# Joint value-output weights split on TensorE and ScalarE, reciprocals moved ahead, in a two-layer gated cross-attention kernel

## The chip, the cores and the metric

The kernel runs on one core of one Trainium2 chip as a single launch. The metric is device time in microseconds (us), the slowest core's, which here is the only one. A core has TensorE (PE, whose weight loads are listed apart as PEld), VectorE (DVE), ScalarE (ACT), GpSimd (POOL) and SyncE (SP), each with its own instruction stream, and DMA queues. They order each other by semaphores.

## The reference, cut to what matters

Two layers of gated cross-attention and feed-forward follow each other on x of shape (16, 128, 256). The change lies in the attention of the second layer:

```python
def _L1_xattn_ref(x, latents, ...):      # x = ctx_1024, latents = layernorm(x of the block)
    B, M, N, DIM, DH, H = (8, 1024, 64, 256, 128, 8)
    xn = _layernorm(x, gamma_media, beta_media)
    ln = _layernorm(latents, gamma_lat, beta_lat)
    q = ln @ Wq + bq
    kv = concatenate([xn, ln], axis=1) @ Wkv + bkv
    k, v = split(kv, 2)
    ... 8 heads of 128, q scaled by 128 ** -0.5
    attn = softmax(q k^T)
    return (attn v).reshape(b, -1, 1024) @ Wo + bo
x = x + tanh(g_xattn[1]) * _L1_xattn_ref(ctx_1024, layernorm(x), ...)
```

The actual batch is 16 with 128 queries and 256 keys (128 of the context, 128 of x). The kernel does not make v: since attn (t Wv) Wo = (attn t)(Wv Wo), it multiplies Wv and Wo once per head into joint weights of 256 x 256 (`nw`), weighs the normed tokens t by attn, and multiplies the result u by the joint weights. The bias of v goes through Wo once and is added to bo.

## The kernel before, in words

All large products take their operands as a high part rounded to the short float format of TensorE (type fp32r) and a low part, which is the remainder, so three matmuls (high high, high low, low high: `PARTS3`) stand for one.

**The entry block** (L1492 to L1553) runs between two barriers of all engines. TensorE multiplies the turned value weights with the raw output weights, two matmuls per head, into one of three PSUM banks `psN` (L1505). ScalarE first rounds the key weights (L1511), then copies each head's product twice: rounded into `nw[0]` (L1514), and whole into `made_nw` (L1515). VectorE scales and splits the query weights (L1531 to L1533), takes the low part of the key weights (L1536), adds the routed rows of the first two batches to x (`combine`, L1469), takes their statistics and norms (`norm_step`, L66 to L95, 15 steps of tiny operations in a chain), and writes the normed rows (L1548, L1552). GpSimd waits for the last stores of the feed-forward before, gathers four batches' rows by indirect DMA (L1465), and then widens the value bias, `bvw` (L1524).

**The main block** works on 8 pairs of batches with 8 heads each, so 64 units, and is software-pipelined by a hand-written order: in step n TensorE does `keys(n)` (L1646), `score(n-1)` (L1665), `queries(n)` (L1655), in the first steps two heads of `values_bias` (L1712), in some steps `turn_kv` of a coming batch (L1637), `output(n-5)` (L1705), `weigh(n-4)` (L1686) and `turn(n-2)` (L1675), the transposes of the probabilities. Step 4 has no `output` yet. Both `turn_kv` and `turn` write the one PSUM bank `psT`, so `turn` waits until the low part of what `turn_kv` left there has been read (`kv_lo`):

```python
def turn(n, turned_kv):
    pe.wait_ge(s["p_done"], n + 1)
    at_least(pe, s["pt_lo"], n)
    at_least(pe, s["kv_lo"], turned_kv)
```

The steps in which this happens are written out in tables; a step counts within its pair (n modulo 8):

```python
NORM_AT, TURN_AT, TOKENS_AT = {2: 0, 4: 1}, {4: 0, 6: 1}, {5: 0, 7: 1}
```

VectorE's order in step n is: low part of k (`keys`, L1872); row maximum of unit n-1 (L1882); low part of q (L1877); in steps 0 to 3 two `lower_product` each, which write `nw[1]` = `made_nw` - `nw[0]` (L1947); in step 3 `sum_bias` (L1952, L1954); in steps 2 and 4 of each of the first seven pairs `later_norm`, which norms a batch of the next pair by four operations of two SBUF inputs (L1475, L1480); in steps 4 and 6 `stage_kv`, the low part of the turned rows (L1867); `normalize(n-1)`, the reciprocal of the exponentials' sums (L1887); `weigh(n-4)` (L1897) and `turn(n-2)` (L1892), again low parts; and last the entering of further batches (L1469, L1921, and links of the norm chain). Each of these waits for its own semaphore, and what stands behind it waits too.

ScalarE's order is high part of k (L1761), of q (L1765), the two exponentials of unit n-1 with their sums (L1771), tokens (L1756), `stage_kv` (L1749), and the high parts of u (L1783) and of the turned probabilities (L1778). GpSimd multiplies the probabilities by the reciprocals (L1833) after VectorE's reciprocal, and gathers, adds the bias to x (L1839) and lowers tokens (L1824) in other steps.

## Time and profile before

| what | value |
|---|---|
| median of 3 runs | 1040.09 us |
| lowest and highest | 1036.69 and 1044.4 us |
| the profiled execution's own time | 1037.69 us |
| its span, first to last instruction | 1035.9 us |
| what lies around the span | 1.79 us |
| mean granted TensorE clock | 0.961 |
| TensorE busy | 943.9 us, 91% |
| VectorE busy | 735.7 us, 71% |
| ScalarE busy | 615.9 us, 59% |
| GpSimd busy | 301.6 us, 29% |

The entry block takes about 319.6 to 333.6 us of the span and the attention's main block 333.6 to about 762 us. Busy shares are means over stages; a stage's own limit is read from its waits. A granted clock of 1.00 is TensorE's upper level, 2.4 GHz, and 0.50 its lower one, 1.2 GHz. In the timeline rows a line has the start, the duration, engine, line of the program, operation, what it writes and reads, shapes and the count of instructions merged in it; a bracket holds the time that the engine sat idle before it and what ended that.

### The profile page before, as it was taken

The page shows a single profiled execution, that of the slowest core. Times are in us where ns is not written, and L with a number is a line of the kernel's source. Part 1 is how long each engine was busy: PE and PEld are TensorE (multiplying, and loading weights), DVE is VectorE, ACT ScalarE, POOL GpSimd, SP SyncE. Part 2 cuts the span into 40 slices and gives each one's busy share as a digit, 9 for nine tenths or more (in the row PEclk, how much of TensorE's full clock was granted, in tenths as well). Part 3 has the DMA queues.
Part 4 walks back from the last instruction along what each step waited for, and adds up shares of the span by engine and source line. Part 5 has one row for each costly group of instructions (what it writes and reads, how often), then busy time and mean ns, then how long its engine had stood idle before and what let it go on. Part 6 is the DMA issues. An engine that isn't in the chain of part 4 may idle for free. (4 is left out here: it accounts for less than half of the span.)

```text
span 1035.9 us, 22000 instructions
## 1 busy us (share of the span) xinstructions
PE 943.9 (91%) x7942; PEld 870.8 (84%) x7942; DVE 735.7 (71%) x1812; ACT 615.9 (59%) x1500; POOL 301.6 (29%) x361
## 2 busy tenths in 40 slices
PE   5899999777997899999999999999988999799993
PEld 4688876776886689999999999999877999799992
DVE  7888888685778878776666565655667876565655
ACT  4688886474987355555555555555555443566560
POOL 3444434035002334222222222131100002466631
PEclk9899999888998899999999999999999999899997
DMA  9511110014731101000000000020051001454417
GB/s 276 197 54 53 64 63 2 1 36 123 210 113 50 39 21 47 1 22 9 14 21 1 22 1 22 1 74 30 2 163 42 1 2 22 118 167 135 132 56 269
DMA packets 64617, 69.24 MB, mean 67 GB/s; under 512 B 11488, under 2 KB 56032, under 8 KB 64384
## 3 DMA queue, kind: packets, MB, share of 16 engines
q1 hardware_dynamic: 57680, 52.22, 16.1%
q0 software_dynamic: 5712, 15.36, 5.4%
q8 instruction: 65, 1.06, 0.4%
q10 hardware_dynamic: 1120, 0.27, 0.1%
q14 instruction: 40, 0.33, 0.1%
HBM read 46.07 MB, written 21.76 MB: 65 GB/s over the span
## 5 line engine op out<-in xcount | busy, mean ns | idle before, releaser
L1833 POOL TENSOR_TENSOR a_probs<-a_probs,a_softmax 128x512 f32<-128x512 f32 x64 | 66.7, 1043 | 296.2 <-DVE a_softmax L1887 296.2
L1646 PE MATMUL a_psK<-a_kvThi,a_wk 128*128 128x512 f32 x256 | 97.4, 421 | 2.5 <-DVE a_klo L1872 2.5
L1897 DVE TENSOR_TENSOR a_ulo<-a_psU,a_uhi 128x512 fp32r<-128x512 f32 x64 | 44.2, 691 | 66.7 <-ACT a_uhi L1783 66.7
L314 POOL TENSOR_SCALAR t_neg<-t_raw,t_nthr 128x256 bf16<-128x256 f32 (+1 forms) x54 | 60.5, 1136 | 103.6 <-DVE t_nthr L557 97.6
L1771 ACT ACTIVATE a_probs<-a_psS,a_softmax 128x256 f32<-128x256 f32 x128 | 59.5, 470 | 34.9 <-DVE a_softmax L1882 34.9
L2420 POOL DMA_INDIRECT rows<-m_tokens,r_comes x40 | 40.4, 1009 | 125.4 <-DVE r_comes L2630 109.8
L1686 PE MATMUL a_psU<-a_pThi,a_tokhi 128*128 128x256 f32 x256 | 72.8, 284 | 2.3 <-DVE a_pTlo L1892 2.3
L1705 PE MATMUL a_psY<-a_nwhi,a_uhi 128*128 128x256 f32 x256 | 73.4, 287 | 1.2 <-DVE a_ulo L1897 1.2
L1686 PE MATMUL a_psU<-a_pThi,a_toklo 128*128 128x256 f32 x256 | 72.4, 283 | 0.0
L1686 PE MATMUL a_psU<-a_pTlo,a_tokhi 128*128 128x256 f32 x256 | 72.4, 283 | 0.0
L1761 ACT ACTIVATE a_khi<-a_psK,a_bk 128x512 fp32r<-128x512 f32 x64 | 44.0, 688 | 47.7 <-PE a_psK L1646 47.4
L1705 PE MATMUL a_psY<-a_nwlo,a_uhi 128*128 128x256 f32 x256 | 72.3, 282 | 0.0
L1705 PE MATMUL a_psY<-a_nwhi,a_ulo 128*128 128x256 f32 x256 | 72.1, 282 | 0.0
L2316 PE MATMUL f_psY<-a_wk,f_g_split 128*128 128x256 f32 x480 | 67.3, 288 | 3.0 <-issue 2.3
L1783 ACT ACTIVATE a_uhi<-a_psU 128x512 fp32r<-128x512 f32 x64 | 38.2, 597 | 52.8 <-PE a_psU L1686 52.1
L1872 DVE SCALAR_TENSOR_TENSOR a_klo<-a_psK,a_bk,a_khi 128x512 fp32r<-128x512 f32 x64 | 47.7, 746 | 25.5 <-ACT a_khi L1761 25.5
L2303 PE MATMUL f_psH<-m_turned,a_wq 128*128 128x320 f32 x384 | 65.5, 318 | 0.0
L2316 PEld LDWEIGHTS f_psY<-a_wk,f_g_split 128*128 128x128 f32 x480 | 59.9, 188 | 4.8 <-issue 3.8
L2673 DVE TENSOR_TENSOR f_g_split<-f_g,f_g_split 128x320 fp32r<-128x320 f32 x64 | 30.4, 490 | 42.1 <-ACT f_g_split L2372 33.3
L1646 PEld LDWEIGHTS a_psK<-a_kvThi,a_wk 128*128 128x128 f32 x256 | 48.9, 191 | 12.7 <-DVE a_klo L1872 3.6
L2366 ACT ACTIVATE f_g<-f_psH,f_xb 128x320 f32<-128x320 f32 x64 | 33.0, 528 | 44.6 <-PE f_psH L2303 33.4
L1765 ACT ACTIVATE a_qhi<-a_psQ,a_bq 128x256 fp32r<-128x256 f32 x64 | 30.3, 473 | 48.3 <-PE a_psQ L1655 48.3
(412 smaller groups left out, 3191.8 us busy)
## 6 DMA issues: line engine op xcount, KB each, us to landing
t_raw<-in_L_ffn_expert_w SPq DMA_DIRECT2D x16, 512.0 KB, 3.5
f_raw<-in_fc_T SPq DMA_DIRECT2D x16, 512.0 KB
m_results<-a_zeros SPq DMA_DIRECT2D x8, 512.0 KB, 3.5
m_sorted<-m_zeros SPq DMA_DIRECT2D x1, 2944.0 KB, 12.6
m_n<-m_sorted SPq DMA_DIRECT2D x23, 128.0 KB, 2.3
m_expert_out<-e_y SPq DMA_DIRECT2D x23, 128.0 KB, 1.7
a_rawkv<-in_L_xattn_Wkv SPq DMA_DIRECT2D x8, 256.0 KB, 5.6
m_n<-in_sh_T SPq DMA_DIRECT2D x2, 1024.0 KB, 8.5
```

The source lines that it names most:

```text
L314: ins = pool.tensor_scalar(neg[:, own], raw[h % NRAW][:, own], nthr[h % 2][:, n:n + 1], None, ALU.is_lt)
L1646: ins = pe.matmul(psK[:].rearrange("p b t -> p (b t)"), wk[x][:, a, h * DH:(h + 1) * DH], kvT[pair % 2][y][:, a, :, :, :].rearrange("p b m ...
L1686: ins = pe.matmul(psU[b][:, f, :], tok[pair % 2][x][:, b, kt, f * P:(f + 1) * P], pT[gr % 2][y][:, b, kt, :, :].rearrange("p h t -> p (h t)"),
L1705: ins = pe.matmul(psY[:, b, :], u[ch % 2][x][:, f, hh * P:(hh + 1) * P], nw[y][:, f, 2 * j + hh, :], start=first, stop=last, skip_group_ch ...
L1761: act.activation(k_[n % 2][0][:], psK[:], ACT.Identity, bias=bk[:, n % NH:n % NH + 1]).then_inc(s["k_hi"], 1)
L1771: act.activation(probs[n % 2][:, b, :], psS[n % 2][:, b, :], ACT.Exp, bias=nmax[:, n % NM, b:b + 1], accum_out=sums[:, n % NM, b:b + 1]).t ...
L1833: pool.tensor_tensor(own, own, rsum[:, n % NM, :].unsqueeze(2).to_broadcast([P, 2, 2 * P]), ALU.mult).then_inc(s["p_done"], 1)
L1872: dve.scalar_tensor_tensor(out=k_[n % 2][1][:], in0=psK[:], scalar=bk[:, n % NH:n % NH + 1], in1=k_[n % 2][0][:].bitcast(F32), op0=ALU.add ...
L1897: dve.tensor_tensor(u[ch % 2][1][:], psU[ch % 2][:], u[ch % 2][0][:].bitcast(F32), ALU.subtract).then_inc(s["u_lo"], 1)
L2303: ins = pe.matmul(psH[k % NG][:, 0:HALF], xw1[e % 2][x][:, a * F + f * P:a * F + (f + 1) * P], xT[e % 2][y_][:, a, rows], start=(n == 0), ...
L2316: ins = pe.matmul(psY[n % 2][:, 0, :], xgs[e % 2][x][:, f, t * P:(t + 1) * P], xw2[e % 2][y_][:, f * D:(f + 1) * D], start=(k == 0), stop= ...
L2420: pool.indirect_dma_start(xin[e % 2][:, t, :], None, xr, bass.IndirectOffsetOnAxis(ap=comes[:, e * NT + t:e * NT + t + 1], axis=0))\
```

## The change

1. In the entry block ScalarE copies each head's product once, rounded (`upper`), TensorE then adds minus that high part to the same PSUM bank (`take_off`, one matmul of 128x512 with `less`, the negated identity, as weights), and ScalarE copies the remainder into `nw[1]` (`lower`). `made_nw` and VectorE's eight `lower_product` are gone, and with them the waits for `n_lo`. VectorE makes `less` as its first instruction.
2. GpSimd widens the value bias ahead of the gathers rather than behind them, and TensorE does the first two heads of `values_bias` at the end of the entry block; the others move one step ahead, so `psY` is allocated earlier.
3. In VectorE's steps the reciprocal `normalize(n-1)` stands directly behind the low part of q, ahead of `sum_bias`, `later_norm` and `stage_kv`.

```diff
@@ -1482,12 +1482,23 @@
             ins.then_inc(normed, 1)
             dve.wait_ge(normed, n)
 
+        psY = ps("a1_psY", [P, 2, D], F32, c)
+        psB = psY[:, 0, :]
         with ExitStack() as r:
             rawq, rawkv, rawo = (begun["weights"][n] for n in ("q", "kv", "o"))
-            made_nw = sb("a1_made_nw", [P, KD, NH, D], F32, r)
+            spare = sb("a1_spare", [P, KD * NH * D - P], F32, r)
+            less = sb("a1_less", [P, P], F32R, r)
             bvw = sb("a1_bvw", [P, NH, P], F32, r)
             psN = [ps(f"a1_psN{i}", [P, KD, D], F32, r) for i in range(3)]
-            names = "k_hi steps combined stats_done n_done n_out centred".split()
+
+            def values_bias(pe, part, done=None):
+
+                for h in (2 * part, 2 * part + 1):
+                    ins = pe.matmul(psB, bvw[:, h, :], rawo[:, h, :], start=(h == 0), stop=(h == NH - 1))
+                if h == NH - 1:
+                    ins.then_inc(done, 1)
+
+            names = "k_hi steps combined stats_done n_done n_hi less_done n_left n_out wide centred".split()
             s = {n: sem(f"a1w_{n}", r) for n in names}
             q_in, kv_in, o_in, small_in = (begun["loaded"][n] for n in ("q", "kv", "o", "small"))
             flat = lambda t: t.rearrange("p a n -> p (a n)")
@@ -1498,34 +1509,59 @@
 
                 @block.tensor
                 def _(pe):
-                    pe.wait_ge(o_in, NH // 2 * 16)
-                    for h in range(NH):
+                    def product(h):
                         at_least(pe, s["n_out"], h - 2)
                         for a in range(KD):
-                            ins = pe.matmul(psN[h % 3][:, a, :], vT[:, h, a * P:(a + 1) * P], rawo[:, h, :], start=True, stop=True)
+                            ins = pe.matmul(psN[h % 3][:, a, :], vT[:, h, a * P:(a + 1) * P], rawo[:, h, :], start=(a == 0), stop=False, skip_group_check=True)
                         ins.then_inc(s["n_done"], 1)
+
+                    def take_off(h):
+                        pe.wait_ge(s["n_hi"], h + 1)
+                        ins = pe.matmul(psN[h % 3][:].rearrange("p a d -> p (a d)"), less[:], nw[0][:, :, h, :], start=False, stop=True,
+                                        skip_group_check=True)
+                        ins.then_inc(s["n_left"], 1)
+
+                    pe.wait_ge(o_in, NH // 2 * 16)
+                    product(0)
+                    pe.wait_ge(s["less_done"], 1)
+                    for h in range(1, NH):
+                        product(h)
+                        take_off(h - 1)
+                    take_off(NH - 1)
+                    pe.wait_ge(s["wide"], 1)
+                    values_bias(pe, 0)
 
                 @block.scalar
                 def _(act):
                     act.wait_ge(kv_in, 2 * NI // D * 16)
                     act.activation(wk[0], rawkv[:, :, 0:NI], ACT.Copy).then_inc(s["k_hi"], 1)
-                    for h in range(NH):
+                    def upper(h):
                         act.wait_ge(s["n_done"], h + 1)
-                        act.activation(nw[0][:, :, h, :], psN[h % 3][:], ACT.Copy)
-                        act.activation(made_nw[:, :, h, :], psN[h % 3][:], ACT.Copy).then_inc(s["n_out"], 1)
+                        act.activation(nw[0][:, :, h, :], psN[h % 3][:], ACT.Copy).then_inc(s["n_hi"], 1)
+
+                    def lower(h):
+                        act.wait_ge(s["n_left"], h + 1)
+                        act.activation(nw[1][:, :, h, :], psN[h % 3][:], ACT.Copy).then_inc(s["n_out"], 1)
+
+                    upper(0)
+                    for h in range(1, NH):
+                        upper(h)
+                        lower(h - 1)
+                    lower(NH - 1)
 
                 @block.gpsimd
                 def _(pool):
+                    pool.wait_ge(small_in, 128)
+                    pool.tensor_copy(bvw[:], bv[:].unsqueeze(2).to_broadcast([P, NH, P])).then_inc(s["wide"], 1)
                     for b in range(2):
                         pool.wait_ge(y_out[b], (NT0 + 1 - b) // 2 * 16)
                     for i in range(SOON):
                         gather(pool, i)
-                    pool.wait_ge(small_in, 128)
-                    pool.tensor_copy(bvw[:], bv[:].unsqueeze(2).to_broadcast([P, NH, P]))
 
                 @block.vector
                 def _(dve):
                     k = Steps(dve, s["steps"])
+                    dve.tensor_scalar(less[:], ident[:], -1.0, None, ALU.mult).then_inc(s["less_done"], 1)
                     dve.wait_ge(small_in, 128)
                     dve.wait_ge(q_in, NI // D * 16)
                     dve.tensor_scalar(bq[:], bq[:], scale, None, ALU.mult)
@@ -1575,15 +1611,12 @@
         psS = [ps(f"a1_psS{i}", [P, 2, 2 * P], F32, c) for i in range(2)]
         psT = ps("a1_psT", [P, 2, 2, P], F32, c)
         psU = [ps(f"a1_psU{i}", [P, KD, 2 * P], F32, c) for i in range(2)]
-        psY = ps("a1_psY", [P, 2, D], F32, c)
         names = ("centred normed resid kv_turned kv_hi kv_lo tok_hi tok_lo k_done k_hi k_lo q_done q_hi q_lo s_done max_done "
                  "exp_done rsum_done p_done t_done pt_hi pt_lo u_done u_hi u_lo y_done x_done const_done zeroed w1_in w2_in w_hi "
-                 "m1_in m1_const stats_done chain combined entered links n_lo b_done b_sum").split()
+                 "m1_in m1_const stats_done chain combined entered links b_done b_sum").split()
         s = {n: sem(f"a1_{n}", c) for n in names}
-        psB = psY[:, 0, :]
         kv_turning = [psT[:], psU[1][:].rearrange("p k (m t) -> p k m t", m=2)]
 
-        PER_UNIT = 2
         rawo = begun["weights"]["o"]
 
 
@@ -1706,16 +1739,9 @@
                                                 start=first, stop=last, skip_group_check=True)
                     ins.then_inc(s["y_done"], 1)
 
-                def values_bias(part):
-
-                    for h in (2 * part, 2 * part + 1):
-                        ins = pe.matmul(psB, bvw[:, h, :], rawo[:, h, :], start=(h == 0), stop=(h == NH - 1))
-                    if h == NH - 1:
-                        ins.then_inc(s["b_done"], 1)
-
                 turn_kv(0, 0)
                 turn_kv(1, 0)
-                values_bias(0)
+                values_bias(pe, 1)
                 for n in range(UNITS):
                     if n < NU:
                         keys(n)
@@ -1723,10 +1749,8 @@
                         score(n - LAG_S)
                     if n < NU:
                         queries(n)
-                    if n < NH // 2 - 1:
-                        values_bias(n + 1)
-                    if n == LAG_Y:
-                        pe.wait_ge(s["n_lo"], NH)
+                    if n < NH // 2 - 2:
+                        values_bias(pe, n + 2, s["b_done"])
                     if coming(n, TURN_AT) is not None:
                         turn_kv(coming(n, TURN_AT), n - LAG_T)
                     if n >= NU and 0 <= n - LAG_U < NCH:
@@ -1744,8 +1768,6 @@
                     pair, bb = divmod(b, 2)
                     act.wait_ge(s["kv_turned"], b + 1)
                     at_least(act, s["q_done"], (pair - 1) * NH)
-                    if b == 2:
-                        act.wait_ge(s["n_lo"], NH)
                     act.activation(kvT[pair % 2][0][:, :, bb, :, :].rearrange("p a m t -> p a (m t)"),
                                    kv_turning[b == 1].rearrange("p a m t -> p a (m t)"), ACT.Copy).then_inc(s["kv_hi"], 1)
 
@@ -1943,10 +1965,6 @@
                     dve.wait_ge(s["chain"], norm_length(0))
                     dve.tensor_scalar(m["rows"][:, b, 0:D], x_sb[:, b, :], x_mean[:, b:b + 1], x_rstd[:, b:b + 1], ALU.subtract, ALU.mult)
 
-                def lower_product(h):
-                    dve.tensor_tensor(nw[1][:, :, h, :], made_nw[:, :, h, :], nw[0][:, :, h, :].bitcast(F32), ALU.subtract)\
-                       .then_inc(s["n_lo"], 1)
-
                 def sum_bias():
                     dve.wait_ge(s["b_done"], 1)
                     dve.tensor_tensor(bo[:], psB, bo[:], ALU.add).then_inc(s["b_sum"], 1)
@@ -1963,17 +1981,14 @@
                         maximum(n - LAG_S)
                     if n < NU:
                         queries(n)
-                    if n * PER_UNIT < NH:
-                        for h in range(n * PER_UNIT, (n + 1) * PER_UNIT):
-                            lower_product(h)
+                    if 0 <= n - LAG_S < NU:
+                        normalize(n - LAG_S)
                     if n == LAG_U - 1:
                         sum_bias()
                     if coming(n, NORM_AT) is not None:
                         later_norm(coming(n, NORM_AT))
                     if coming(n, TURN_AT) is not None:
                         stage_kv(coming(n, TURN_AT))
-                    if 0 <= n - LAG_S < NU:
-                        normalize(n - LAG_S)
                     if 0 <= n - LAG_U < NCH:
                         weigh(n - LAG_U)
                     if 0 <= n - LAG_T < NU:
```

## Rows read from the trace of the kernel before

**Rows 1.** Waits from 372 to 762 us: engine, line, releaser: total us, times, longest.

```profile
PE a_psT L1675 <- DVE a_kvTlo L1867: 3.0, 8, 0.5
```

**Rows 2.** Timeline of VectorE in step 20 (463.5 to 471 us), as described above.

```profile
464.98 0.75 DVE L1872 SCALAR_TENSOR_TENSOR a_klo<-a_psK,a_bk,a_khi 128x512 fp32r<-128x512 f32 x1 [0.64 <-ACT a_khi L1761]
...
466.63 0.47 DVE L1475 SCALAR_TENSOR_TENSOR a_centred<-rows,mean,a_gam 128x256 f32<-128x256 f32 x1
...
468.45 0.69 DVE L1867 TENSOR_TENSOR a_kvTlo<-a_psT,a_kvThi 128x512 fp32r<-128x512 f32 x1
469.06 0.15 DVE L1887 RECIPROCAL a_softmax<-a_softmax 128x2 f32<-128x2 f32 x1
```

**Rows 3.** Timeline of ScalarE in step 20: the end of the exponentials.

```profile
467.18 0.20 ACT L1771 ACTIVATION_READ_ACCUMULATOR a_probs<-a_psS,a_softmax 128x1 f32 x1
```

**Rows 4.** Timeline of TensorE in step 20: last matmul before its wait, and after.

```profile
468.66 0.28 PE L1686 MATMUL a_psU<-a_pThi,a_toklo 128*128 128x256 f32 x1
469.29 0.63 PE L1675 MATMUL a_psT<-ident,a_probs 128*128 128x128 f32 x4 [0.35 <-DVE a_kvTlo L1867]
```

**Rows 5.** Timeline of VectorE and GpSimd, 327 to 356 us: operations that overlap.

```profile
327.10 1.57 DVE L73 TENSOR_TENSOR mean<-stats 128x2 f32<-128x2 f32 x1
...
327.59 1.05 POOL L1524 COPY a_bvw<-a_bv 128x1024 f32<-128x1024 f32 x1
...
348.28 1.20 POOL L1833 TENSOR_TENSOR a_probs<-a_probs,a_softmax 128x512 f32<-128x512 f32 x1 [7.74 <-DVE a_softmax L1887]
...
355.52 1.04 POOL L1833 TENSOR_TENSOR a_probs<-a_probs,a_softmax 128x512 f32<-128x512 f32 x1 [4.91 <-DVE a_softmax L1887]
...
355.94 0.90 DVE L1469 SCALAR_TENSOR_TENSOR x_sb<-m_n,m_prob,x_sb 128x256 f32<-128x256 f32 x1
```

**Rows 6.** Timeline of TensorE around two waits in steps 2 and 4.

```profile
345.99 0.51 PE L1646 MATMUL a_psK<-a_kvThi,a_wk 128*128 128x512 f32 x1 [1.80 <-DVE a_klo L1872]
...
367.10 0.63 PE L1675 MATMUL a_psT<-ident,a_probs 128*128 128x128 f32 x4 [1.42 <-DVE a_kvTlo L1867]
```

**Rows 7.** Windows: length, busy by engine (count), PEclk, DMA share, GB/s.

```profile
344.00:348.00 4.00, 2.20 (x8) 1.61 (x8) 3.79 (x13) 1.02 (x4) 0.00 (x0) 0.87 0.00 0
348.00:352.00 4.00, 4.00 (x23) 3.80 (x22) 3.76 (x14) 1.19 (x3) 2.17 (x2) 0.70 0.12 33
```

**Rows 8.** Timeline of the entry block and the barrier behind it.

```profile
319.77 1.22 DVE L1532 TENSOR_SCALAR a_wq<-a_rawq 128x2048 fp32r<-128x2048 f32 x1
...
320.79 1.10 POOL L1465 DMA_INDIRECT m_n<-m_expert_out,m_pos  x1 [64.31 <-DMA m_expert_out<-e_y]
...
333.65 1.09 PE L1637 MATMUL a_psT<-ident,a_kv 128*128 128x128 f32 x4 [5.14 <-PEq L1494]
```

**Rows 9.** The page's costliest groups: count, busy us, mean ns, idle before.

```profile
L1646 PE MATMUL a_psK<-a_kvThi,a_wk 128*128 128x512 f32 x256 | 97.4, 421 | 2.5 <-DVE a_klo L1872 2.5
```

**Rows 10.** Timeline of VectorE in steps 0 to 4.

```profile
340.49 1.28 DVE L1947 TENSOR_TENSOR a_nwlo<-a_made_nw,a_nwhi 128x512 fp32r<-128x512 f32 x2
...
345.19 0.74 DVE L1872 SCALAR_TENSOR_TENSOR a_klo<-a_psK,a_bk,a_khi 128x512 fp32r<-128x512 f32 x1
...
348.04 0.16 DVE L1887 RECIPROCAL a_softmax<-a_softmax 128x2 f32<-128x2 f32 x1
...
350.59 0.75 DVE L1872 SCALAR_TENSOR_TENSOR a_klo<-a_psK,a_bk,a_khi 128x512 fp32r<-128x512 f32 x1
...
355.27 0.17 DVE L1887 RECIPROCAL a_softmax<-a_softmax 128x2 f32<-128x2 f32 x1
...
357.22 0.73 DVE L1872 SCALAR_TENSOR_TENSOR a_klo<-a_psK,a_bk,a_khi 128x512 fp32r<-128x512 f32 x1
...
360.77 0.16 DVE L1887 RECIPROCAL a_softmax<-a_softmax 128x2 f32<-128x2 f32 x1
...
362.72 0.73 DVE L1872 SCALAR_TENSOR_TENSOR a_klo<-a_psK,a_bk,a_khi 128x512 fp32r<-128x512 f32 x1
...
366.26 0.69 DVE L1867 TENSOR_TENSOR a_kvTlo<-a_psT,a_kvThi 128x512 fp32r<-128x512 f32 x1
```

## The prediction

> **What bounds the kernel now.** I read the waits from 372 to 762 us first, where the attention runs evenly. TensorE's only wait that comes back there is the one of the probability transposes for the low part of the turned rows, 8 times, 3.0 us in all [rows 1]; otherwise it goes from matmul to matmul, so that whatever makes that wait longer lengthens the kernel. Then the timeline of one step with that wait, step 20: TensorE runs out of matmuls at 468.94 (468.66 plus 0.28) and starts the transposes at 469.29, 0.35 us later, behind VectorE's low part that began at 468.45 [rows 2, 4]. The same low part ends the 1.42 us wait at 367.10 [rows 6]. Last the entry: in steps 0 to 4 VectorE has one operation behind the other, and TensorE waits for its low parts of k [rows 6, 10]. So VectorE's order bounds the first 30 us, and TensorE bounds the rest with one thin place per pair.
>
> **Part 1, the lower products leave VectorE (steps 0 to 3).** Two take 1.28 us [rows 10], start to start with what follows 1.20. Eight are 4.8 us less work, but the steps also wait for the exponentials, which nothing fills any more. From the start of the low part of k to the reciprocal it takes at least 2.43 us where the exponentials end last: in step 20 from 464.98 to their end at 467.38, plus 0.03 to react [rows 2, 3]. With that, in times of the trace before:
> - step 1: low part of k at 345.19 - 1.20 = 343.99; reciprocal at 346.42 instead of 348.04, so 1.62 gained; next low part of k at 350.59 - 1.62 = 348.97.
> - step 2: reciprocal at 351.40 instead of 355.27. Behind it now stand the four norm operations, 1.82 us (466.63 to 468.45 in step 20) plus the collision priced in part 3, 0.77 us, and then the old distance to the next low part of k, 357.22 - 355.27 = 1.95, less the 0.43 by which an entering batch was held in it (0.90 against 0.47 for an operation of the same form [rows 2, 5]). That gives 351.40 + 1.82 + 0.77 + 1.52 = 355.51, a gain of 1.7.
> - step 3: reciprocal at 357.94; the bias sum (0.7) now behind it; next low part of k at about 360.4 instead of 362.72 (between 360.2 and 360.7, as the bias's second operation is held or not): 2.3 gained.
> - step 4: reciprocal at 362.8, norm and collision behind it, low part of the turned rows at 365.5 instead of 366.26. **Gain 0.75 us** where TensorE takes over as the bound.
>
> The waits for the lower products themselves (TensorE in step 5, ScalarE for batch 2) had ended long before and bring nothing.
>
> **Part 2, the entry block.** TensorE gets eight more matmuls of 128x512 at 0.42 us or less and two heads of the bias sum, about 1.0 us: 4.4 us, and it stood idle for 5.14 us before the next block [rows 8, 9]; ScalarE's copies stay sixteen. I cost this at nothing, hidden by VectorE's norm chain; if that cover went, up to 1 us. `less` adds about 0.15 us (nearest row: small operations 0.16) to VectorE's chain. The bias copy leaves the place where it held a 128x2 addition for 1.57 us instead of 0.16, which such small operations take [rows 5, 10]: 1.4 us back. At its new place, the block's start, it meets VectorE's query scaling (1.22 us) and, right behind, operations with two inputs; the gathers wait for their own stores until 320.79, so a copy of 1.05 us from about 319.6 is nearly over by then [rows 8]. If they collide, VectorE or the gathers lose up to 1.05. Bounds: 1.25 gained, or 0.2 gained, or 0.9 lost if the gathers are late as well; I take **0.3 gained**, since the nearest row (copy against VectorE) is a full hold. The page "SBUF — State Buffer" of the Trainium skill (section "Who interferes with whom") says that VectorE in a two-port mode, too, shuts GpSimd out of the shared ports for a whole instruction or is shut out; by it the copy is only moved from one collision to the next, and by the other reading, no collision with a one-input operation, the block would gain the 1.25. No row before shows that pair.
>
> TensorE is busy until shortly before the barrier now, so its first transposes may run at the upper clock: 1.09 us for four before, 0.63 elsewhere [rows 4, 8]. Two sets of them lie in the path with ScalarE between; I take **0.6 gained**, 0 to 0.7.
>
> **Part 3, the reciprocal first, in the evenly running part.** In steps without a norm nothing changes: the reciprocal waited for the exponentials already. In step 20 it stood behind norm and low part at 469.06. Now it waits until 467.41, the norm begins at 467.50 instead of 466.63, and the low part of the turned rows, still behind the norm, starts **0.87 us later**: a wait once filled by the norm is now empty. Then GpSimd's multiplication starts 0.25 us behind the reciprocal (348.04 to 348.28) and runs beside the norm. Rows 5 show what that does: with both engines on two SBUF inputs, an entering batch begun at 355.94 ended at 356.84, 0.28 after GpSimd's 356.56, in 0.90 instead of 0.47; the 128x2 addition ended with GpSimd's copy; and GpSimd's 1.20 instead of 1.04 shows it getting in as soon as the running VectorE operation ends. So the second norm operation is held: reciprocal + 1.44 + 0.28 = 1.72 for its end instead of 0.95, **0.77 us more**. From below it is 0, if VectorE keeps its ports from one operation to the next; from above 1.04, GpSimd's whole operation. I take 0.77, the nearest rows. Together 1.64 us more of TensorE waiting in steps 12, 20, 28, 36, 44 and 52: **9.8 us lost**. Nothing absorbs it. The steps 2 (modulo 8) push the low parts of u and p back by about 1.1 us, but TensorE reads those only in its next step, behind keys, score and queries; I cost it at nothing. Steps 6 have no norm, and their reciprocal goes into the wait for ScalarE's copy: nothing. That the reciprocal comes earlier is worth nothing here, since no transpose waits for the multiplication.
>
> **Part 4, the clock.** TensorE's wait in those six steps grows from 0.35 to 2.0 us. After the gap of 1.80 us at 345.99 its clock fell to the lower level, the windows show 0.87 and 0.70; the missing clock is 4 x 0.13 + 4 x 0.30 = 1.7 us [rows 6, 7]. After 1.42 us the transposes ran at 0.63 as elsewhere, so it did not [rows 4, 6]. A gap of 2.0 lies above the one that brought a fall; not each need do so. I take two falls of six, 3.4 us lost (bounds 0 and 10.3). In step 4 TensorE, done early with its work, stands idle for 5 us before 365.5; I count one fall there, 1.7 us lost.
>
> **Sum** against the profiled execution's own 1037.69: -0.3 - 0.6 - 0.75 + 9.8 + 3.4 + 1.7 = +13.2, 1050.9. The median shown is 1040.09, 2.4 above that execution, with 7.7 between lowest and highest; I put the forecast between the two bases, **1052**. It is a loss of a bit over 1%, which is also about what a measurement of this kernel can tell from no change (10.4 us).
>
> **Rivals.**
> - *Only the empty wait counts.* No hold between norm and multiplication, stalls of 1.2 us, too short for the clock to fall (1.42 did not do it). Then 6 x 0.87 = 5.2 lost, and the entry gains 0.3 + 0.6 + 0.75 + 2 x 0.77 = 3.2, less one fall, 1.7: +3.7, 1041.4, on the median 1043.8. For it: no row shows several VectorE operations in a row with GpSimd waiting. Against: GpSimd's 1.20.
> - *Not slower: the low part of the turned rows is not pushed.* Place: step 4 of each pair. It decides when the exponentials end before VectorE is done with q, 467.38 against 466.7 in step 20; the reciprocal would then be free. With VectorE's lighter entry this could hold if scores came 0.7 us earlier against it. Then only the entry counts: -0.3 - 0.6 - 2.3, 1034.5, on the median 1036.9. Against: TensorE sets the distance of the steps, and the row maximum follows the low part of k in both orders.
> - *Every stall lowers the clock.* 6 falls: -1.65 + 9.8 + 10.3 + 1.7 = +20.2, 1057.9, on the median 1060.3.
> - *The change doesn't do what it says:* the moved copy delays gathers or the added matmuls outlast VectorE, the entry gives nothing back. Up to 3 us above the forecast's sum, 1054.
>
> **How the numbers follow.** Forecast 0.56 (1046 to 1056 on its own), empty wait alone 0.17, not slower 0.12, every stall 0.11, entry gives nothing 0.04. The range of 8 in 10 leaves out the not slower case and the end of the every-stall case: 1039 to 1061. Above 1050.5 lie the forecast with at least one fall in the six steps, the every-stall case and the one where the entry gives nothing: 0.50. Below 1029.7 nothing I can build, 0.03. Within 1%: 0.47.
>
> **What would show it.** The norm's first operation in step 20 right behind the reciprocal, the second one of 1.2 us instead of 0.47; TensorE's waits for the low part of the turned rows at about 2 us, six times, 12 in all; granted clock under 1.00 at some of the six steps; in the entry the 128x2 addition of 0.16. Wrong would be: those waits unchanged (the not slower case), or at 1.2 us with short norm operations (only the empty wait).

## The result, and the profile after

| | before | changed |
|---|---|---|
| median of 20 runs | 1042.35 us | 1058.25 us |
| lowest to highest | 1034.66 to 1051.87 | 1048.08 to 1067.57 |
| span of the profiled execution | 1035.9 | 1057.0 |

The ratio is 1.0148, 95% interval 1.0126 to 1.0171: slower, as forecast, by 15.9 us between the medians where the sum had 13.2 and the forecast 1052. The ratio leaves out slow runs, those over 1.5% above the fastest of their kernel, and so is not exactly the quotient of the two medians.

The two traces were laid side by side at four marks. Before the entry block the changed trace is 2.0 us later, in work that the change does not touch. The entry block, first matmul to first transposes behind the barrier, is 13.62 us instead of 14.03. The main block, from there to the start of the last output matmul, is 440.66 instead of 424.52, so **16.1 us** of the 21.1 between the two spans are in it. Behind it the traces differ by another 3.4, again in untouched work. The two blocks that the change touches thus lose 15.7 us, close to the 15.9 between the medians; the other 5.4 belong to this pair of executions.

The waits of the changed kernel from 372 to 780 us, for the row in [rows 1] (total us, times, longest):

```profile
PE a_psT L1708 <- DVE a_kvTlo L1889: 12.3, 6, 2.2
```

The step with turned rows and a norm, step 20. VectorE's timeline, for [rows 2]:

```profile
470.96 0.48 DVE L1899 SCALAR_TENSOR_TENSOR a_qlo<-a_psQ,a_bq,a_qhi 128x256 fp32r<-128x256 f32 x1
472.13 0.17 DVE L1909 RECIPROCAL a_softmax<-a_softmax 128x2 f32<-128x2 f32 x1 [0.70 <-ACT a_probs L1793]
472.24 0.48 DVE L1475 SCALAR_TENSOR_TENSOR a_centred<-rows,mean,a_gam 128x256 f32<-128x256 f32 x1
472.64 1.26 DVE L1475 SCALAR_TENSOR_TENSOR a_centred<-x_sb,mean,a_gam 128x256 f32<-128x256 f32 x1
473.94 0.48 DVE L1480 SCALAR_TENSOR_TENSOR a_kv<-a_centred,rstd,a_bet 128x256 f32<-128x256 f32 x1
...
474.85 0.69 DVE L1889 TENSOR_TENSOR a_kvTlo<-a_psT,a_kvThi 128x512 fp32r<-128x512 f32 x1
```

GpSimd beside it:

```profile
472.37 1.25 POOL L1855 TENSOR_TENSOR a_probs<-a_probs,a_softmax 128x512 f32<-128x512 f32 x1 [3.83 <-DVE a_softmax L1909]
```

TensorE in the same step, for [rows 4]:

```profile
473.38 0.28 PE L1719 MATMUL a_psU<-a_pThi,a_toklo 128*128 128x256 f32 x1
475.69 0.63 PE L1708 MATMUL a_psT<-ident,a_probs 128*128 128x128 f32 x4 [2.03 <-DVE a_kvTlo L1889]
```

VectorE's `a_centred` and `a_kv` operations are the norm, `a_kvTlo` is the low part of the turned rows. VectorE sits idle for 0.70 us between q and the reciprocal, its first norm operation takes 0.48, the second 1.26. GpSimd's multiplication ends at 473.62, and the second norm operation 0.28 later, at 473.90. The long form stands in all 14 norms of the trace. TensorE's wait is 2.03 instead of 0.35.

The windows of the changed kernel around the waits that end at 421.90, 475.69 and 529.37 (columns as in [rows 7], PEclk the third from the end):

```profile
416.00:420.00 4.00, 3.75 (x32) 3.54 (x31) 3.30 (x7) 2.20 (x7) 1.24 (x1) 1.00 0.12 33
420.00:424.00 4.00, 2.10 (x8) 1.84 (x9) 2.92 (x7) 0.98 (x2) 0.00 (x0) 0.78 0.00 0
424.00:428.00 4.00, 4.00 (x26) 3.71 (x26) 3.92 (x9) 1.53 (x3) 0.00 (x0) 0.80 0.00 0
476.00:480.00 4.00, 4.00 (x18) 3.57 (x17) 3.13 (x7) 1.28 (x2) 0.00 (x0) 0.60 0.00 0
532.00:536.00 4.00, 4.00 (x36) 4.00 (x36) 2.58 (x7) 2.40 (x8) 0.61 (x1) 1.00 0.02 4
```

Behind the first two the clock went to the lower level; the missing clock of the first is 4 x (0.22 + 0.20) = 1.7 us. Behind the third it did not. In one-microsecond windows it fell behind four of the six waits (about 422, 476, 582 and 688 us), at 367 us, in step 4, and at 357 us, where it also fell in the kernel before. Why it stayed up behind the other two waits, which are as long, no run here shows.

The entry block's small operations and the copy, VectorE first, for [rows 5, 8]:

```profile
321.62 1.10 DVE L1564 TENSOR_SCALAR a_less<-ident 128x128 fp32r<-128x128 f32 x1 [0.79 <-PEq L1230]
...
330.09 0.16 DVE L73 TENSOR_TENSOR mean<-stats 128x2 f32<-128x2 f32 x1
```

GpSimd:

```profile
321.61 1.03 POOL L1555 COPY a_bvw<-a_bv 128x1024 f32<-128x1024 f32 x1 [63.16 <-POOLq L1230]
```

The addition that had been held for 1.57 us is 0.16, but `less` now takes 1.10 and ends with the copy (322.72 and 322.64). Behind the barrier TensorE's first transposes run at the upper level:

```profile
335.24 0.63 PE L1670 MATMUL a_psT<-ident,a_kv 128*128 128x128 f32 x4 [2.07 <-PEq L1505]
```

VectorE in steps 1 to 4, for [rows 10]; to compare, take off the 1.59 us by which the main block starts later:

```profile
344.87 0.75 DVE L1894 SCALAR_TENSOR_TENSOR a_klo<-a_psK,a_bk,a_khi 128x512 fp32r<-128x512 f32 x1
...
349.86 0.75 DVE L1894 SCALAR_TENSOR_TENSOR a_klo<-a_psK,a_bk,a_khi 128x512 fp32r<-128x512 f32 x1
...
356.47 0.73 DVE L1894 SCALAR_TENSOR_TENSOR a_klo<-a_psK,a_bk,a_khi 128x512 fp32r<-128x512 f32 x1
...
361.70 0.73 DVE L1894 SCALAR_TENSOR_TENSOR a_klo<-a_psK,a_bk,a_khi 128x512 fp32r<-128x512 f32 x1
...
366.84 0.69 DVE L1889 TENSOR_TENSOR a_kvTlo<-a_psT,a_kvThi 128x512 fp32r<-128x512 f32 x1
```

### The profile page after: what moved, and what is told of

Same layout as the page of the kernel before. It is cut to its first block and busy times, and to the rows that moved or that the text cites. A ratio compares the mean times of both kernels' runs of the same rounds, so it can differ in the third digit from the quotient of the medians.

```text
span 1057.0 us, 22014 instructions
## 1 busy us (share of the span) xinstructions
PE 953.5 (90%) x7950; PEld 878.6 (83%) x7950; DVE 742.5 (70%) x1805; ACT 617.3 (58%) x1500; POOL 306.1 (29%) x361
## 3 DMA queue, kind: packets, MB, share of 16 engines
q1 hardware_dynamic: 57680, 52.22, 16.1%
## 5 line engine op out<-in xcount | busy, mean ns | idle before, releaser
L1855 POOL TENSOR_TENSOR a_probs<-a_probs,a_softmax 128x512 f32<-128x512 f32 x64 | 69.6, 1088 | 310.2 <-DVE a_softmax L1909 310.2
L1679 PE MATMUL a_psK<-a_kvThi,a_wk 128*128 128x512 f32 x256 | 100.3, 433 | 3.3 <-DVE a_klo L1894 2.6
L2318 PEld LDWEIGHTS f_psH<-m_turned,a_wq 128*128 128x128 f32 x384 | 59.2, 195 | 0.0
```

Of the source, the lines that this page charges most:

```text
L1679: ins = pe.matmul(psK[:].rearrange("p b t -> p (b t)"), wk[x][:, a, h * DH:(h + 1) * DH], kvT[pair % 2][y][:, a, :, :, :].rearrange("p b m ...
L1855: pool.tensor_tensor(own, own, rsum[:, n % NM, :].unsqueeze(2).to_broadcast([P, 2, 2 * P]), ALU.mult).then_inc(s["p_done"], 1)
L2318: ins = pe.matmul(psH[k % NG][:, 0:HALF], xw1[e % 2][x][:, a * F + f * P:a * F + (f + 1) * P], xT[e % 2][y_][:, a, rows], start=(n == 0), ...
```

## The experiments

Two things had to be separated: whether the order on VectorE or the rebuilt entry costs the time, and what the 2.0 us wait is made of and leads to. The first four runs were timed beside the kernel before at a median of 1042.75 us, the other four later, beside the same kernel at 1028.95 us; so medians are compared only within a group, and ratios across the two. Lengths of the main block are from one profiled execution of each kernel, between the same marks; before is 424.52, changed 440.66. The clock differs from one execution to the next (its mean was 0.942 to 0.961 in the 20 times of the changed kernel), so a difference of one fall, about 1.5 us, between two such lengths says little.

**Only the order put back.**

```diff
 # VectorE's steps of the changed kernel
-                    if 0 <= n - LAG_S < NU:
-                        normalize(n - LAG_S)
                     if n == LAG_U - 1:
                         sum_bias()
                     if coming(n, NORM_AT) is not None:
                         later_norm(coming(n, NORM_AT))
                     if coming(n, TURN_AT) is not None:
                         stage_kv(coming(n, TURN_AT))
+                    if 0 <= n - LAG_S < NU:
+                        normalize(n - LAG_S)
```

> The changed kernel with only VectorE's order put back: the reciprocal again behind the bias sum, the norm and the low part of the turned rows. Theory (the reciprocal's place is the loss, the new entry a small gain): the six waits of TensorE for the low part of the turned rows are 0.35 us again, no clock fall between 410 and 740 us, 1 to 5 us below the kernel before, ratio 0.995 to 0.999. Rival (the rebuilt entry, its added matmuls and the moved bias copy cost the time): waits may shrink, but the time stays 8 us or more above the kernel before, ratio 1.008 or more.

Measured: 1039.59 us median, ratio 0.9972 (0.9939 to 1.0005), main block 421.38. The waits from 372 to 760 us:

```profile
PE a_psT L1708 <- DVE a_kvTlo L1889: 3.1, 8, 0.6
```

The waits and the clock between 410 and 740 us are those of the kernel before. The rebuilt entry is not the loss; in the profile it is a gain of 3.5 us (0.35 in the entry block, 3.14 in the main block), which the timed runs do not tell from no change.

**Only the reciprocal moved**, the same swap the other way, in the kernel before, behind the lower products.

```diff
 # VectorE's steps of the kernel before
+                    if 0 <= n - LAG_S < NU:
+                        normalize(n - LAG_S)
                     if n == LAG_U - 1:
                         sum_bias()
                     ...
                         stage_kv(coming(n, TURN_AT))
-                    if 0 <= n - LAG_S < NU:
-                        normalize(n - LAG_S)
```

> The kernel before with only VectorE's reciprocal moved ahead of the bias sum, the norm and the low part of the turned rows; lower products, copies and bias copy as before. Theory: six waits of about 2.0 us in place of 0.35, three to five falls of the clock, together 15 to 19 us lost, ratio 1.014 to 1.018. Rival (entry costs): ratio under 1.005.

Measured: 1062.83 us median, ratio 1.0188 (1.0143 to 1.0233), a little above the expected 1.014 to 1.018, main block 444.16. The waits from 372 to 780 us:

```profile
PE a_psT L1675 <- DVE a_kvTlo L1867: 12.3, 6, 2.2
```

The same six waits, and the clock fell behind the same four of them. The swap by itself is the whole loss and more: the other parts of the change had hidden some 3.5 us of it (444.16 against 440.66).

**The multiplication held back** until the norm is done, so that the two do not meet.

```diff
 # GpSimd, changed kernel
                 def normalize(n):
                     pool.wait_ge(s["rsum_done"], n + 1)
+                    if coming(n + 1, NORM_AT) is not None:
+                        pool.wait_ge(s["normed"], coming(n + 1, NORM_AT) - 1)
```

> The changed kernel, but in the steps with a norm GpSimd's multiplication waits until VectorE's norm is done, so the two never meet on SBUF. Theory (of the 1.68 us of added wait 0.87 is the empty wait for the exponentials and 0.8 is VectorE held behind GpSimd): the six waits are 1.2 us, no norm operation over 0.5 us, and the clock does not fall in those steps, since 1.42 us did not lower it before; 6 x 0.8 + 4 x 1.7 = 11.6 us below the changed kernel, ratio to before 1.002 to 1.006. Rival (no hold; the wait for the exponentials is all): waits stay 2.0, ratio 1.013 to 1.017.

Measured: 1045.16 us median, ratio 1.0017 (0.9981 to 1.0053), main block 429.12, 11.5 us below the changed kernel where 11.6 were expected. VectorE in step 20:

```profile
469.47 0.17 DVE L1911 RECIPROCAL a_softmax<-a_softmax 128x2 f32<-128x2 f32 x1 [0.70 <-ACT a_probs L1793]
469.58 0.48 DVE L1475 SCALAR_TENSOR_TENSOR a_centred<-rows,mean,a_gam 128x256 f32<-128x256 f32 x1
469.99 0.48 DVE L1475 SCALAR_TENSOR_TENSOR a_centred<-x_sb,mean,a_gam 128x256 f32<-128x256 f32 x1
...
471.42 0.69 DVE L1891 TENSOR_TENSOR a_kvTlo<-a_psT,a_kvThi 128x512 fp32r<-128x512 f32 x1
```

TensorE in the same step:

```profile
472.25 0.63 PE L1708 MATMUL a_psT<-ident,a_probs 128*128 128x128 f32 x4 [1.25 <-DVE a_kvTlo L1891]
```

The second norm operation is 0.48 again and the wait 1.25: of the 2.03, 0.35 was there before, 0.90 is the empty wait for the exponentials, and 0.78 is VectorE held behind GpSimd. In all 14 norms of this trace the second operation takes 0.48. At 1.25 (1.36 once) the clock fell nowhere between 372 and 760 us.

**Work in the gap.** Six matmuls whose product nobody reads, ahead of the transposes.

```diff
 # TensorE, changed kernel; filler(n) repeats the six matmuls of keys(n) into psK, after k_lo of n
+                    if n >= NH and coming(n, NORM_AT) is not None and coming(n, TURN_AT) is not None:
+                        filler(n)
                     if 0 <= n - LAG_T < NU:
                         turn(n - LAG_T, turned_before(n + 1))
```

> The changed kernel with six more matmuls of 128x512 (a repeat of the unit's key product, 1.4 us of work that nobody uses) ahead of the transposes in the six steps with the long wait. Theory (the wait lets the clock fall): the gap shrinks from 2.03 to about 0.6 us, the transposes start at the same time after the matmuls before them, and the four falls between 420 and 700 us are gone; 6.8 us below the changed kernel, ratio to before 1.006 to 1.010, although TensorE does 8.6 us more work. Rival (the falls have another cause): four falls stay, ratio 1.013 to 1.017; if the extra matmuls delay the step, more.

Measured: 1055.34 us median, ratio 1.0109 (1.0057 to 1.0162), main block 435.78. TensorE in step 20:

```profile
476.44 0.40 PE L1746 MATMUL a_psK<-a_kvThi,a_wk 128*128 128x512 f32 x1
477.48 0.63 PE L1708 MATMUL a_psT<-ident,a_probs 128*128 128x128 f32 x4 [0.63 <-DVE a_kvTlo L1899]
```

The windows behind the first two waits:

```profile
424.00:428.00 4.00, 3.40 (x24) 3.17 (x25) 3.12 (x7) 1.29 (x2) 0.00 (x0) 1.00 0.00 0
476.00:480.00 4.00, 3.37 (x20) 2.66 (x19) 3.12 (x6) 1.15 (x3) 0.00 (x0) 1.00 0.00 0
```

The transposes still wait for VectorE, so nothing is gained in the steps themselves; but the clock stays at 1.00 behind all six waits. In the main block 4.9 us come back, of 6 that the four falls cost; the rest is 0.6 before the first wait, where this execution's first transposes took 1.09 us at the lower clock level, and a new wait of 0.56 for GpSimd in step 14. The timed ratio lies a little above the expected 1.006 to 1.010 and its interval overlaps the changed kernel's; what shows the cause is the trace, not the timing.

**The low part ahead of the norm.**

```diff
 # VectorE's steps of the changed kernel, the reciprocal stays first
-                    if coming(n, NORM_AT) is not None:
-                        later_norm(coming(n, NORM_AT))
                     if coming(n, TURN_AT) is not None:
                         stage_kv(coming(n, TURN_AT))
+                    if coming(n, NORM_AT) is not None:
+                        later_norm(coming(n, NORM_AT))
```

> The changed kernel with one swap on VectorE: in the steps with both, the low part of the turned rows goes ahead of the norm; the reciprocal stays first. Theory (TensorE waits for nothing but that low part, and the held norm hurts nobody): the six waits go from 2.03 us to 0 to 0.1, no clock fall between 420 and 700 us, 16 to 20 us below the changed kernel, ratio to before 0.993 to 0.998. Rival (the held norm then makes the low parts behind it late for TensorE): new waits for the low parts of u, p or k of 0.5 us or more in those steps, ratio 1.002 or more.

Measured: 1024.29 us median, ratio 0.9975 (0.9944 to 1.0006), main block 421.98. TensorE no longer waits for that low part. Two smaller waits are new: 0.2 us six times, for VectorE's residual addition, and two for GpSimd's multiplication, 1.9 in all. So the 2.2 us of the six old waits come back as 3.3 us of new ones, and the main block is no shorter than with the whole old order (421.38): this order removes the loss and adds no gain that the runs show.

**The same, and the norm first where no rows are turned.**

```diff
 # VectorE's steps of the run before this one
-                    if 0 <= n - LAG_S < NU:
+                    if coming(n, TURN_AT) is not None and 0 <= n - LAG_S < NU:
                         normalize(n - LAG_S)
                     if n == LAG_U - 1:
                         sum_bias()
                     if coming(n, TURN_AT) is not None:
                         stage_kv(coming(n, TURN_AT))
                     if coming(n, NORM_AT) is not None:
                         later_norm(coming(n, NORM_AT))
+                    if coming(n, TURN_AT) is None and 0 <= n - LAG_S < NU:
+                        normalize(n - LAG_S)
```

> As the run with the low part ahead of the norm, but in the steps with a norm and no turned rows (2 modulo 8), and in step 3, the reciprocal stands last as in the kernel before, so that the norm fills the wait for the exponentials and does not meet the multiplication. Theory (in the evenly running part those steps cost nothing either way; in step 2 of the entry VectorE is the bound): 1 to 2 us below the run with the low part ahead of the norm in the first five steps only, ratio to before 0.991 to 0.997. Rival (the first reciprocals pay in the entry): equal or slower than that run.

Measured: 1024.10 us median, ratio 0.9950 (0.9917 to 0.9983), main block 420.00. It is the only kernel here whose whole interval lies under 1, but the interval overlaps that of the old order (0.9939 to 1.0005). Its main block is 2.0 us shorter than that of the run before (1 to 2 were expected), all of it by step 4: the transposes there start 28.2 us into the block instead of 30.2. The old order's trace has a clock fall in step 4, about 1.5 us, and this one has not; that alone is as much as the 1.4 us between their main blocks (421.38 and 420.00), so a gain over the old order is not shown. Its step 20, VectorE:

```profile
461.30 0.17 DVE L1909 RECIPROCAL a_softmax<-a_softmax 128x2 f32<-128x2 f32 x1 [0.70 <-ACT a_probs L1793]
461.79 0.69 DVE L1889 TENSOR_TENSOR a_kvTlo<-a_psT,a_kvThi 128x512 fp32r<-128x512 f32 x1 [0.32 <-ACT a_kvThi L1771]
462.39 0.48 DVE L1475 SCALAR_TENSOR_TENSOR a_centred<-rows,mean,a_gam 128x256 f32<-128x256 f32 x1
```

and TensorE:

```profile
462.54 0.28 PE L1719 MATMUL a_psU<-a_pThi,a_toklo 128*128 128x256 f32 x1
462.66 0.60 PE L1708 MATMUL a_psT<-ident,a_probs 128*128 128x128 f32 x4
```

The low part is done at 462.48, before TensorE comes for the bank, and the norm is not held, though it begins at 462.39, 0.2 us before the multiplication ends (462.59).

**The reciprocal first only where no rows are turned.**

```diff
 # VectorE's steps of the changed kernel
-                    if 0 <= n - LAG_S < NU:
+                    if coming(n, TURN_AT) is None and 0 <= n - LAG_S < NU:
                         normalize(n - LAG_S)
                     ...
                         stage_kv(coming(n, TURN_AT))
+                    if coming(n, TURN_AT) is not None and 0 <= n - LAG_S < NU:
+                        normalize(n - LAG_S)
```

> The changed kernel with the old order in the steps that stage turned rows and the reciprocal first in the others. Theory (only the steps with turned rows and a norm cost time): in steps 10, 18 and so on the second norm operation takes 1.26 us in place of 0.48 and TensorE does not wait, the six waits are 0.35 us, ratio to before 0.996 to 1.001, within 2 us of the run with the whole old order. Rival (the hold costs in every step where it happens): six more waits in steps 2 modulo 8, ratio 1.004 or more.

Measured: 1030.24 us median, ratio 1.0018 (0.9990 to 1.0046), a little above the expected 0.996 to 1.001, main block 422.57. VectorE in step 18:

```profile
450.38 1.26 DVE L1475 SCALAR_TENSOR_TENSOR a_centred<-x_sb,mean,a_gam 128x256 f32<-128x256 f32 x1
```

TensorE in step 20:

```profile
463.86 0.63 PE L1708 MATMUL a_psT<-ident,a_probs 128*128 128x128 f32 x4 [0.36 <-DVE a_kvTlo L1889]
```

VectorE is held in each of the seven steps with a norm and no turned rows, and behind the entry no wait of TensorE follows: the same 0.78 us costs something only where a wait ends with it. In the entry VectorE's order does cost: the transposes of step 4 start 31.5 us into the main block instead of 28.8. Some 0.6 of these 2.7 us may be the first transposes, which took 1.09 us here and 0.63 there, and 1.5 are made up again behind step 4, where the clock fell in the old order's trace and not in this one; that leaves 1.2 us over the old order's main block.

**The bias copy back behind the gathers**, with the old order on VectorE.

```diff
 # GpSimd, entry block
-                    pool.wait_ge(small_in, 128)
-                    pool.tensor_copy(bvw[:], ...).then_inc(s["wide"], 1)
                     for b in range(2):
                         pool.wait_ge(y_out[b], ...)
                     for i in range(SOON):
                         gather(pool, i)
+                    pool.wait_ge(small_in, 128)
+                    pool.tensor_copy(bvw[:], ...).then_inc(s["wide"], 1)
```

> The run with the whole old order, but GpSimd widens the value bias behind the gathers again, as before. Theory (moving the copy moved a collision): the first small VectorE operation of the entry block, 1.10 us behind the copy in the changed kernel, takes about 0.2, and the norm chain's first addition takes 1.2 to 1.6 us again, so the block is 0.3 to 0.6 us longer than 13.68. Rival (no collision at the start, the copy's move is pure gain): the block is 1.2 us or more longer.

There is one execution, so no ratio: the entry block is 14.12 us instead of 13.68. VectorE in it:

```profile
319.49 0.23 DVE L1564 TENSOR_SCALAR a_less<-ident 128x128 fp32r<-128x128 f32 x1 [0.80 <-PEq L1230]
...
327.11 1.51 DVE L73 TENSOR_TENSOR mean<-stats 128x2 f32<-128x2 f32 x1
```

and GpSimd:

```profile
327.54 1.05 POOL L1559 COPY a_bvw<-a_bv 128x1024 f32<-128x1024 f32 x1
```

With the copy first, `less` pays 0.87 us; with it last, the norm chain pays 1.35. The move trades one collision for a cheaper one and nets 0.44 us.

## Why the prediction was right, point by point

**The empty wait and the hold: right, in size and place.** Worked out: 0.87 + 0.77, a second norm operation of about 1.2, a wait of 2.0. Measured: 0.90 + 0.78, 1.26, and a wait of 2.03 or 2.04 (2.15 the first time), six times. Six times 1.68 is 10.1 us against the 9.8 of the sum. The run with the multiplication held back separates the two terms, and the one with only the reciprocal moved shows that nothing else of the change is needed for the loss.

**The clock: the mechanism right, the size too small.** The step of the sum that was mis-sized is "two falls of six, 3.4 us". There were four, in two separate traces behind the same four waits. "Two of six" rested on one gap of the trace before, 1.80 us; that trace has a second one, 1.87 us, which ends at 356.61 in step 3, and the clock fell behind it too (PEclk 0.61 from 357 to 358, 0.50 behind), while the 1.42 us in step 4 brought none. So both gaps of the main block near 2 us had brought a fall, and those rows spoke for more than two of six. Four is no fixed number either: the 20 times of the changed kernel run from 1048 to 1068 us.

Each fall made the distance from one such step's transposes to the next one's longer by about 1.5 us (53.7 where it fell, 52.15 where not, 50.47 before), so together 6 us rather than 3.4. The main block's 16.1 are then 10.1 of waits, 6 of these falls and 1.5 of step 4's, less 1.0 of the entry and 0.5 of a wait in step 14 that is gone. That the waits cause the falls is shown from both sides, six waits in one trace each: at 1.25 us of wait there was none, and with matmuls in the gap, the transposes starting as late as before, none either.

**The entry: right within half a microsecond.** The block gained 0.41 where 0.3 was taken. Behind it the low parts of k, less the 1.59 us, stand at 343.3, 348.3, 354.9 and 360.1; worked out, with the 0.6 for the warm start, were 343.4, 348.4, 354.9 and 359.8. The low part of the turned rows in step 4 stands at 365.25, worked out 364.9, so this part gained 1.0 instead of 1.35. The 0.3 us were lost in step 3, where the second operation of the bias sum was held behind GpSimd, 0.91 us instead of 0.35; the prediction had this as the far end of its bounds. The 0.6 for the warm start was in part luck: in three other traces with `take_off` in the entry block (work in the gap, the reciprocal first only where no rows are turned, the copy back) the first transposes took 1.09 us again.

The fall of the clock in step 4 came too, at 367 us, behind a wait of 3.9 us where 5 had been expected. Against the gain of 1.0 it cost about 1.5, so with the new order the lighter entry brought nothing by the end of that fall. With the old order the same low part lets the transposes start 28.8 us into the main block instead of 33.5.

**What was costed at nothing** was nothing: the added matmuls ended before VectorE's chain (TensorE still waited 2.07 at the barrier), in the evenly running part the norm of steps 2 modulo 8 was held and nobody waited, and the earlier reciprocal had no taker there, where no wait of the kernel before was for the multiplication.

The sum was made on the profiled execution, 1037.69; on the 20-run median of 1042.35 the same 13.2 gives 1055.6, and the 2.7 us missing to 1058.25 are of the size of the two falls too few, 3 us. None of the rivals stands: the run in which the empty wait is alone has a ratio of 1.0017, the changed kernel 1.0148; the not slower case falls with the wait of 2.03; the clock fell behind four waits, not six; and the entry block became 0.41 us shorter, with gathers no later against the block's start (1.19 us behind it, 1.17 before), so it did give something back.

## What to carry to other kernels

Behind an operation that waits for another engine, look at what stands in front of it: an in-order engine that is idle until then can hold work there for free, and moving the waiting operation ahead puts that work behind the wait. Moving it earlier only pays if its result has a waiting reader; here the reader that waited was of another result. Putting that one first took the wait away and won back the whole loss (main block 421.98 against 440.66), but no more than the old order did (421.38). Where TensorE is the bound, price a new gap not by its length alone: where the clock fell behind it, 1.68 us more of gap cost 3.2 here.

## What the runs showed of the hardware that was not expected

An operation of one SBUF input was held as well: the negation of 128x128 took 1.10 us beside GpSimd's copy and 0.23 without it. The page "SBUF — State Buffer" of the Trainium skill (section "Who interferes with whom") says that a VectorE operation in a two-port mode and a GpSimd operation shut each other out for a whole instruction. The trace agrees as to the hold: `less` ended at 322.72, the copy at 322.64; in which mode the negation ran, no trace shows. Statistics of 128x256 were not held. In the kernel before one ran in its usual 0.43 us while the multiplication of 348.28 to 349.48 was under way:

```profile
348.62 0.43 DVE L1921 BATCH_NORM_STATS2 stats<-x_sb 128x6 f32<-128x256 f32 x1
```

GpSimd also came in between two norm operations that VectorE had back to back, in every norm where the two met (14 in the changed trace), with the same 1.26 us each time. The prediction had left open whether VectorE would keep its ports there.
